# W1's last four tiles folded by ScalarE and the vector engine, W2's high parts rounded by ScalarE, one router event

## The reference

```python
xr = rotate(q_left, q_right, x) * gate
probs = softmax(xr @ Wr.T)
h = gelu(xr @ W1[7] + b1[7])            # 256 -> 1024
y = (h @ W2[7] + b2[7]) * probs[:, 7:8] # 1024 -> 256
out = x + y
```

## Time and profile before

| | us |
|---|---|
| median of 3 runs | 103.41 (103.25 to 103.62) |
| the profiled execution | 103.47 |
| its span in the trace | 101.4 |
| TensorE busy | 97.7 (96%) |
| vector engine busy | 67.2 (66%) |
| ScalarE busy | 53.8 (53%) |
| POOL busy | 28.0 (28%) |

### The profile page before, as it was taken

One profiled execution on the slowest core, in us unless ns is written; L12 is line 12 of the kernel. 1 busy time (PEld: TensorE's weight loads), 2 busy tenths in 40 slices (PEclk: granted clock), 3 DMA queues, 4 the chain that ended last, 5 costly groups with the idle time before them and its releaser, 6 DMA issues.

```text
span 101.4 us, 1451 instructions
## 1 busy us (share of the span) xinstructions
PE 97.7 (96%) x516; PEld 81.5 (80%) x516; DVE 67.2 (66%) x131; ACT 53.8 (53%) x89; POOL 28.0 (28%) x21
## 2 busy tenths in 40 slices
PE   6999999999999999999999999999999999999990
PEld 7679888778888888888888888788888888888980
DVE  1579689999940789486623695466922666599551
ACT  1467695854434955774408944854408944453600
POOL 3300054001999950000000000089998000000000
PEclk9999999999999999999999999999999999999999
DMA  2999999991000000129334100000054000007105
GB/s 65 311 246 250 209 221 214 222 187 25 0 0 0 0 6 1 5 54 211 150 84 99 26 1 0 6 0 0 0 119 90 1 0 0 6 5 176 26 20 187
DMA packets 20246, 8.17 MB, mean 81 GB/s; under 512 B 17808, under 2 KB 18704, under 8 KB 20240
## 3 DMA queue, kind: packets, MB, share of 16 engines
q1 hardware_dynamic: 19520, 7.30, 34.6%
q10 hardware_dynamic: 720, 0.79, 2.4%
HBM read 5.97 MB, written 2.10 MB: 80 GB/s over the span
## 4 chain that ended last, share of the span: by engine, by line
PE 93%; DMA 2%; DVE 2%; DVEq 0%; issue 0%
PE pre L842 41%; PE acc L865 21%; PE acc L869 11%; PE acc L879 4%; PE acc L887 4%; PE pre L806 3%; PE acc L761 2%; PE lT_bank L795 2%; DMA quats<-in_small 2%; PE acc L883 1%; PE acc L881 1%; DVE y L666 1%; PE acc L777 1%; PE lT_bank L777 1%; DVEq L75 0%; PE acc L771 0%
## 5 line engine op out<-in xcount | busy, mean ns | idle before, releaser
L430 ACT ACTIVATE h_hi<-pre,quats 128x512 fp32r<-128x512 f32 x32 | 22.1, 690 | 36.1 <-PE pre L842 33.9
L599 DVE TENSOR_TENSOR h_lo<-h_all,h_hi 128x512 fp32r<-128x512 f32 x32 | 22.0, 688 | 25.7 <-ACT h_all L432 25.7
L865 PE MATMUL acc<-h_hi,w_parts 128*128 128x512 f32 x96 | 25.7, 389 | 0.0
L842 PE MATMUL pre<-xT_hi,w_hi 128*128 128x512 f32 x60 | 23.6, 394 | 0.0
L842 PE MATMUL pre<-xT_lo,w_hi 128*128 128x512 f32 x60 | 23.4, 391 | 0.0
L373 POOL TENSOR_TENSOR exps<-e_const,shifted 128x32 f32<-128x32 f32 x4 | 22.3, 5580 | 0.2
L432 ACT ACTIVATE h_all<-pre,quats 128x512 f32<-128x512 f32 x32 | 21.9, 684 | 0.0
L865 PEld LDWEIGHTS acc<-h_hi,w_parts 128*128 128x128 f32 x96 | 18.0, 188 | 3.7
L842 PE MATMUL pre<-xT_hi,w_lo 128*128 128x512 f32 x60 | 18.5, 390 | 0.0
L869 PE MATMUL acc<-h_lo,w_parts 128*128 128x512 f32 x48 | 14.8, 389 | 0.0
L842 PEld LDWEIGHTS pre<-xT_hi,w_hi 128*128 128x128 f32 x60 | 11.3, 188 | 2.6 <-issue 0.4
(11 more groups left out here) (87 smaller groups left out, 87.6 us busy)
## 6 DMA issues: line engine op xcount, KB each, us to landing
x_sq<-in_x SPq DMA_DIRECT2D x12, 128.0 KB, 4.5
w<-in_W SPq DMA_DIRECT2D x4, 256.0 KB, 6.4
w_last<-in_W_rest SPq DMA_DIRECT2D x4, 256.0 KB, 5.6
out<-out_sq SPq DMA_DIRECT2D x8, 128.0 KB, 2.7
x_sq<-in_x SPq DMA_DIRECT2D x8, 64.0 KB, 5.3
x_last<-in_x SPq DMA_DIRECT2D x1, 512.0 KB, 3.9
out<-out_sq SPq DMA_DIRECT2D x8, 64.0 KB, 2.2
w_first<-in_W_first ACTq DMA_DIRECT2D x2, 132.0 KB, 2.8
```

The costliest lines, as they stand in the source:

```text
L430: nc.scalar.activation(h_hi[:, s, :], pre_bank(b, f)[:, :], ACT.Gelu, bias=b1_cols[:, f:f + 1]).then_inc(h_hi_ready, 1)
L599: nc.vector.tensor_tensor(h_lo[:, s, :], h_all[:, s, :], h_hi[:, s, :].bitcast(F32), ALU.subtract).then_inc(h_lo_ready, 1)
L842: last = nc.tensor.matmul(bank[:, :], w[:, k, cols], part_of_x[:, k, :], start=(n == 0), stop=(n == len(steps) - 1))
L865: nc.tensor.matmul(sums(b, k), w2_parts[:, f, i, k * P:(k + 1) * P], h_hi[:, s, :], start=(f == 0 and i == 0), stop=False)
```

## The change

Chunk 2's columns become two pieces of 128 columns, `w1_mid` (tile 4) and `w1_late` (tile 5), which are loaded four times over and folded as chunk 3 was. The first of the four components is now multiplied by ScalarE for all three pieces. W2's high parts are rounded by ScalarE. TensorE's `fold(2)` is gone. The opening uses the low part of x's first half before it begins the second half. The router runs once for all four blocks, in block 1 after tile 5, for which x of blocks 2 and 3 is turned earlier, each block in a buffer of its own. The weighing, adding and spreading move to other places, and y_sq has two buffers.

```diff
 # SP
-            sp.dma_start(w1_rest[:, 1, :, :], W1_rest[1]).then_inc(w1_loaded[2], 16)
             load_w2(0)
+            sp.dma_start(column_quats[:, :], columns).then_inc(columns_loaded, 16)
+            load_components(w1_mid, W1_mid, w1_loaded[MID_W1])      # 4 DMAs of 128 KB
+            load_components(w1_late, W1_late, w1_loaded[LATE_W1])   # 4 DMAs of 128 KB
             load_w2(1)
+            load_components(w1_last, W1_last, w1_loaded[LAST_W1])   # 4 DMAs of 256 KB, as before
+            load_w2(2)
             load_squares(1)
-            (column_quats, w1_last, load_w2(2))
             load_w2(3)
...
 # ScalarE
+            def first_component(i, piece, total, begun):
+                act.wait_ge(column_M_ready, 1)
+                act.wait_ge(w1_loaded[i], 16 * QUADS)
+                for k in range(KC):
+                    nc.scalar.activation(total[:, k, :], piece[:, 0, k, :], ACT.Copy,
+                                         scale=column_M[:, k, 0:1]).then_inc(begun, 1)
+            def w2_high(i):
+                act.wait_ge(w2_loaded[i], 16)
+                nc.scalar.activation(w2_parts[:, tiles, 0, :], w2[:, tiles, :], ACT.Copy).then_inc(w2_hi_ready, 1)
...
+            w2_high(0)
                     gelu(b, f)
                     if b == 0 and f == 0:
-                        split_w1(2)
+                        first_component(MID_W1, w1_mid, w1_mid_sum, w1_mid_begun)
+                    if b == 0 and f == 1:
+                        mid_w1_high()
+                        first_component(LATE_W1, w1_late, w1_late_sum, w1_late_begun)
+                        w2_high(1)
+                    if b == 0 and f == 3:
+                        late_w1_high()
+                        first_component(LAST_W1, w1_last, w1_last_sum, w1_last_begun)
+                    if b == 0 and f == 4:
+                        w2_high(2)
+                        last_w1_high()
+                    if b == 0 and f == 6:
+                        w2_high(3)
-                    if f == 4 and b < LAST:
+                    if f == (5 if b == 0 else 4) and b < LAST:
                         (split_x(b + 1, k) for both k)
...
 # vector engine, block 0 (each x_low waits for ScalarE's x_high)
                 low_hidden(b, 0)
-                    split_w1(2)
+                    sum_mid_w1(0)      # component 1: 2 adds of 128 elements
+                    sum_mid_w1(1)      # components 2 and 3: 4 adds
                 low_hidden(b, 1)
+                    mid_w1_low()
+                    sum_late_w1(0)
                     split_w2(1)        # without its cast
                 low_hidden(b, 2)
-                    turn_x(1)
+                    sum_late_w1(1)
                 low_hidden(b, 3)
-                    sum_last_w1()
+                    late_w1_low()
+                    sum_last_w1(0)
+                    sum_last_w1(1)
                 low_hidden(b, 4)
                     last_w1_low()
                     split_w2(2)
-                    logits_of(0)
+                    turn_x(1)
                 low_hidden(b, 5)
                     (split_x(1, k) for both k, split_w2(3))
...
 # vector engine, later: turn_x(2) after low 2 and turn_x(3) after low 3 of block 1; all_logits after
 # low 5 of block 1; probability(0) ends block 1, (1), (2), (3) after low 2, 4, 6 of block 2;
 # weigh(0), add_x(0), weigh(1), add_x(1) after low 3, 4, 5, 7 of block 2
 # TensorE
-                    if half == 0:
-                        fold(2)
-                for f in range(2):
-                    for half in range(2):
-                        pe.wait_ge(first_xT_lo_ready, KC * (half + 1))
+                    pe.wait_ge(first_xT_lo_ready, KC * (half + 1))
+                    for f in range(2):
                         last = products(w1_hi, xT_lo, half, f, ends=(half == 1))
...
-                if b == 0 and f % 2 == 0:
-                    pe.wait_ge(w1_lo_ready, f // 2)
+                if b == 0:
+                    pe.wait_ge(w1_lo_ready, max(i for i, (first, _) in enumerate(PIECES) if first <= f))
...
-                    if b % 2 == 0 and f == 4:
-                        router(b // 2)
+                    if b == 1 and f == 5:
+                        router()
```

More of the change, by code:

```diff
@@ L36, in rotation_terms, with adaln_ffn @@
     return component, sign
-def adaln_ffn(nc, x, small, columns, W1_first, W1_rest, W2, b2, out):
+def adaln_ffn(nc, x, small, columns, W1_first, W1_second, W1_mid, W1_late, W1_last, W2, b2, out):
     n_batch, n_seq, C = x.shape
@@ L150, in adaln_ffn @@
         yT = sb("yT", [P, KC, BLOCK])
-        y_sq = sb("y_sq", [P, SQUARES, LANES])
+        y_sq = [sb(f"y_sq{i}", [P, SQUARES, LANES]) for i in range(2)]
         weighed = sb("weighed", [P, SQUARES, LANES])
@@ L365, in _ @@
                                     ALU.add).then_inc(column_M_ready, 1)
[L366 to L374, removed]
+            pool.wait_ge(max_ready, 1)
+            nc.gpsimd.tensor_tensor(shifted[:, :, :], logits,
+                                    logit_max[:, :].unsqueeze(2).to_broadcast([P, N_BLOCKS * TT, NE]),
+                                    ALU.subtract).then_inc(shifted_ready, 1)
+            pool.wait_ge(shifted_ready, 1)
+            for b in range(N_BLOCKS):
+                nc.gpsimd.tensor_tensor(exps[b][:, :, :], e_const[:, :].unsqueeze(2).to_broadcast([P, TT, NE]),
+                                        shifted[:, b * TT:(b + 1) * TT, :], ALU.pow).then_inc(exps_ready, 1)
         @block.scalar
@@ L524, in split_x @@
                 nc.vector.scalar_tensor_tensor(
-                    out=xT_lo[b % 2][:, k, :], in0=xT[b % 2][:, k, :], scalar=scale[:, k:k + 1],
+                    out=xT_lo[b % 2][:, k, :], in0=xT[b][:, k, :], scalar=scale[:, k:k + 1],
                     in1=xT_hi[b % 2][:, k, :].bitcast(F32), op0=ALU.mult, op1=ALU.subtract).then_inc(xT_lo_ready, 1)
@@ L553, in take_router, with second_w1_low, add_components @@
                                         ALU.mult).then_inc(wr_ready, 1)
-            def split_w1(i):
-                dve.wait_ge(w1_hi_ready, i)
-                nc.vector.tensor_tensor(w1_lo[:, :, chunk(i)], fold_banks[i], w1_hi[:, :, chunk(i)].bitcast(F32),
+            def second_w1_low():
+                dve.wait_ge(w1_hi_ready, 1)
+                nc.vector.tensor_tensor(w1_lo[:, :, chunk(1)], fold_bank, w1_hi[:, :, chunk(1)].bitcast(F32),
                                         ALU.subtract).then_inc(w1_lo_ready, 1)
[L560 to L567, removed]
+            def add_components(piece, total, half, begun, added):
+                for o in (1,) if half == 0 else (2, 3):
@@ L568, in sum_last_w1 @@
                     for k in range(KC):
-                        dve.wait_ge(w1_last_added, KC * (o - 1) + k + 1)
+                        if o == 1:
+                            dve.wait_ge(begun, k + 1)
+                        else:
+                            dve.wait_ge(added, KC * (o - 2) + k + 1)
                         nc.vector.scalar_tensor_tensor(
-                            out=w1_last_sum[:, k, :], in0=w1_last[:, o, k, :], scalar=column_M[:, k, o:o + 1],
-                            in1=w1_last_sum[:, k, :], op0=ALU.mult, op1=ALU.add).then_inc(w1_last_added, 1)
+                            out=total[:, k, :], in0=piece[:, o, k, :], scalar=column_M[:, k, o:o + 1],
+                            in1=total[:, k, :], op0=ALU.mult, op1=ALU.add).then_inc(added, 1)
@@ L609, in probability @@
                 dve.wait_ge(exps_ready, b + 1)
-                nc.vector.tensor_reduce(exp_sum[:, :], exps[b % 2][:, :, :], AX.X, ALU.add).then_inc(sum_ready, 1)
+                nc.vector.tensor_reduce(exp_sum[:, :], exps[b][:, :, :], AX.X, ALU.add).then_inc(sum_ready, 1)
                 dve.wait_ge(sum_ready, b + 1)
@@ L627, in turn_sums @@
                     rows = slice(h * SQUARES // n_parts, (h + 1) * SQUARES // n_parts)
-                    last = nc.vector.transpose(y_sq[:, rows, k::KC].rearrange("p (s j) c -> p j s c", j=j),
+                    last = nc.vector.transpose(y_sq[b % 2][:, rows, k::KC].rearrange("p (s j) c -> p j s c", j=j),
                                                yT[:, k, tokens].rearrange("p (j t s) -> p j s t", j=j, s=QUADS))
@@ L923, in _ @@
             turn_first_x()
-            fold(1)
+            second_fold()
             opening()
```

202 lines of the change are left out of this document (123 added, 79 removed).

## The result

| | us | |
|---|---|---|
| the changed kernel, median of 6 runs | 106.19 (105.46 to 107.19) | ratio 1.026 (95%: 1.022 to 1.030) |
| the kernel before, same series | 103.26 | |
| the changed kernel again, 5 runs, another series | 105.61 (105.27 to 105.88) | ratio 1.020 (1.016 to 1.024) |
| the kernel before, that series | 103.57 | |

By the medians the kernel became slower by 2.9 us in the first series and by 2.0 in the second; 105.1 had been forecast. The profiled execution of the first series (107.19 us) fell into a state with a lower TensorE clock, which the ratio leaves out. So I read the repeat beside it, whose profiled execution took 105.27 us at a clock of 1.00: 1.8 us above the 103.47 of before. It is the shortest of the repeat's five executions.

A forecast was written before the change was run, and what follows sets the result against it. TensorE was taken to bound the kernel, holding 93% of the chain of waits. To 103.47 us came -0.61 - 0.4 + 0.88 + 1.54 + 0.29 = +1.7, so 105.2, stated as 105.1; range 103.0 to 106.3.

The forecast's parts named there:

- The mechanism: In block 0 TensorE wants its weights earlier, while ScalarE and the vector engine deliver them late: stalls of 2.7 us.
- the likeliest case: Whole kernel: TensorE's savings are outweighed by stalls for weights in block 0; 104.2 to 105.9 us, chance 0.58.
- rival 1: Block 0, tile 6: the last piece's load lands at 20.5, not 19.3; stall 2.7, total 106.3 us; chance 0.08.
- Fold and opening, -0.61: Block 0's opening: without chunk 2's fold, but with a new 0.24 wait, tile 2 starts at 10.59, before 11.20.
- Router, -0.4: One event of 64 passes in block 1 takes 2.02 us in place of 2.42 for two in blocks 0 and 2.
- Tile 5, +0.88: Block 0: tile 5's weight comes late, so TensorE starts it at 19.63 against 18.75, a stall of 0.88 us.
- the line: Vector engine's add time drawn through two measured widths, 484 ns at 256 elements and 757 at 512: 347 at 128.
- rival 2: Block 0: narrow operations cost in proportion to width (pitch 0.20); smaller stalls, +0.6, total 104.1 us; chance 0.11.
- Tile 6, +1.54: Block 0: TensorE starts tile 6 at 23.89 against 22.35, its weight waiting for the load; 1.1 at least with load early.
- W2's last pair, +0.29: Block 0: turning block 1's x delays the high part of W2's last two tiles; TensorE starts at 29.62 against 29.33.
- Later blocks, nothing: After block 0: earlier x transposes (2.1 us), one exps chain, spreading DMAs and output stores were to cost nothing.

The follow-up runs named there:

- the kernel with the later load: The changed kernel with W2's tiles 4 and 5 (256 KB) loaded ahead of W1's last piece, not behind; ratio 1.022 (1.016 to 1.027) to the kernel before.
- the matmuls on zeros: The changed kernel with matmuls on zeros added in block 0, 4 ahead of tile 5 and 12 ahead of tile 6; ratio 1.026 to the kernel before.

## Why the prediction was right, step by step

The mechanism, its places and the sign were right, the size too small: +1.7 forecast, +2.0 and +2.9 by the medians. The +1.8 between two profiles at full clock is in part luck, as the repeat's profiled execution is the shortest of its five. The first series' median, 106.19, lies outside the likeliest case (104.2 to 105.9) and only 0.1 inside the range's upper end, close to the 106.3 of rival 1.

- **Fold and opening, -0.61.** Measured -0.81 in the repeat and -0.54 in the first profile. The term was taken as more certain than it is: the wait for xT_lo was costed at 0.24 from one trace in which the fold hid it. TensorE's idle time there was 0.23 to 1.17 without the fold, so the term is anything from -0.8 to 0.0 (tile 2 at 10.39 to 11.16, before 11.20).
- **Router, -0.4.** The 64 passes lie 1.88 in the chain, and the product behind them has 0.23 more: 2.11 for 2.46, -0.35. The forecast reckoned the stalls with the router gone from block 0, so its sum is sound. But -0.4 is not what the move is worth in any kernel: alone in the kernel before it cost 0.9.
- **Tile 5, +0.88.** 0.82, and 0.1 for the first product behind a wait, which lasts 0.50 and not 0.40. The adds of 128 elements took 347 to 349 ns in the repeat, against 484 at 256; the line had said 347. Six took 1.66. So rival 2, a cost in proportion to the width, is out. The Trainium skill's rule of a fixed cost per instruction (VectorE: DVE Perf Modes, The TRN2 errata) agrees with these rows.
- **Tile 6, +1.54.** 1.65 in the repeat and 2.05 in the first profile, again with 0.1. The forecast had ScalarE start with the load at 19.34 and TensorE at 23.89. The repeat has 19.37 and 23.89, the first profile 20.05 and 24.57. That the repeat met it to the hundredth is luck, since the load's landing swung from before 18.75 to 20.05 with the same queue. With tile 5's load left out tile 6 lost 1.16, and 1.1 had been the forecast least. Rival 1 (the load at 20.5) is in the first profile, at about 0.6 of its size.
- **W2's last pair, +0.29.** 0.16, and 0.14 in the slower product: 0.30.
- **Later blocks, nothing.** From the start of block 1 to TensorE's last matmul the repeat takes 0.89 more than before, which is the router's 2.11 less the 1.23 of block 2's event. The vector engine did wait 1.8 us for stores of the first output block, as was reckoned, and nothing followed from it.
- **Not in the forecast: the clock.** The fall of the clock in block 0 was seen in the first profile only, not in the repeat's, and the five other runs of that series have 105.46 to 106.27 with clocks of 0.998 and more. It doesn't explain the median. By the ratios that series lies 0.6 us above the repeat, with intervals that overlap; a load that lands later, as in its one profile, would do it, but that is not shown.

## What to carry to other kernels

Work that moves off the bounding engine changes two times at once: the bounding engine needs its next operands earlier, and the engines that took the work deliver them later. Write out both, in the order in which the queues issue, before adding up what was saved. Ask of each operation that is moved away from the bounding engine whose lateness it had covered: the router event was worth -0.35 where the next weight was early, and +0.9 where it was not. Where one trace shows an operand ready just before its use, another run can have it later: here one load with the same queue ahead of it landed before 18.75 in one profile and at about 20.0 in another.

## What the runs showed of the hardware

- TensorE's granted clock can fall to half (1.2 GHz of 2.4) in the middle of a kernel. In the kernel with 1 MB ahead of the last piece TensorE was idle from 22.94 to 28.44; the clock fell at about 26.5 and came back at about 33.3, behind 4.9 us of work at half clock. In the first profile of the changed kernel TensorE was idle for 0.66 ahead of tile 5 and 1.89 ahead of tile 6, and the clock fell at about 25.0, 0.4 us after the work had begun again, and came back at about 28.4. With 0.65 and 2.17 us of idling in the kernel with the later load it did not fall. So the length of the single wait does not decide it. The Trainium skill (TensorE: Matmul & The Clock Gate, The HAM clock gate) has half rate as the default state and activity as what releases it; the trace agrees for the long wait.
- The first matmul of 512 columns behind a wait is followed 0.33 to 0.34 us later by the next, not 0.23, also at full clock (19.39 and 19.73 in the repeat). The same distance stands behind a router event (20.49 and 20.82 in the kernel before) and behind the matmuls on zeros (19.43 and 19.76), so it does not take idling.
- Matmuls of fp32 zeros, 128 x 128 x 128, took 0.108 us per pass back to back (24 passes in 2.60 us), where a pass of 512 columns in fp32r takes 0.23: a quarter of the columns for nearly half the time.
- POOL's five small operations on the columns took 1.65 us from first start to last end in the first profile, at 7.79, and 2.65 in the kernel before, at 13.66. The operations are the same; what slows them at the later place was not tried.
